# A new order of the same instructions on all five queues of a two-layer kernel

## The chip, the cores and the metric

The kernel runs on one core of one Trainium2 chip. The metric is the device time of one execution in microseconds (us). Before the change the median of three runs is 381.72 us (380.91 to 382.23).

## What is computed

Eight sequences of 256 tokens with 128 channels (2048 tokens) go through two layers. In short:

```python
xn = layernorm(x)                       # layer 0
q, k, v = xn@Wq+bq, xn@Wk+bk, xn@Wv+bv  # 16 query heads of 8, 4 key/value heads
x = x + (softmax(q k^T / sqrt(8)) v)@Wo + bo + (g1+g2) * (relu(xn@w1)@w2)   # top-2 gates, one shared expert
xn = layernorm(x)                       # layer 1: state-space block and ternary FFN
xs, z = split(xn@W_in);  xs = silu(causal_conv4(xs));  dt = softplus(xs@W_dt + b_dt);  Bs = xs@W_x
h_t = h_{t-1} * exp(-A dt_t) + Bs_t     # 256 channels x 16 states, scanned over the tokens
y = (sum_s h_t + D*xs) * silu(z)
f = silu(s1*xn@w1) * (s2*xn@w2);  f = gelu(h1s*f@h1);  f = gelu(h2s*f@h2)   # 128 -> 512 -> 512 -> 512
x = x + y@W_out + s3*f@w3
```

In the changed kernel nothing of this is computed in another way.

## The kernel before

Each engine runs one fixed list of *pieces*. A piece is a small function that waits for its semaphores and issues one to ten instructions. The lists stand in `ORDERS` (lines 72 to 126), one string per queue: `3*S` means three S pieces, and the n-th S in the string gets n as its argument. `run_order` (line 129) walks the string. An engine never leaves its list's order, so a piece that waits holds up everything behind it on its engine. A piece is named here with its number, from 0: second4, D39.

**Layer 0** works by batch b of 256 tokens (8 of them). TensorE (PE): `xn_transposes` (438), `project` (458), `v_gate` (429), `S` (317: scores for the row maxima, two 48-row matmuls of 256 columns, 16 a batch), `max_rows` (421), `A` (337: scores again, one 51-row matmul of 512 columns, on the other half of the array's rows), `pv` (349), `heads`, `back`, `proj_out` (the output projection), `ffn_in`, `ffn_out`. 44 `warm` pieces (450) are matmuls on a constant, whose results nobody uses. ScalarE (ACT): `E` (546), the Exp of an A bank; `qk_out`, `relu`, `xn_out`, `o_out`, `normalised`. VectorE (DVE): `M` (586), the maxima of an S bank. GpSimd (POOL): `G` (the gates), `qk_split`, `maxima_split`. SyncE: `put`, `fetch`, `stack` and `rows` move q, k and the maxima through HBM, `loads` brings in layer 1's weights; `decay_rates` on ACT (1085) needs the first two of these loads.

**Layer 1** works by group g of 512 tokens (4 of them). PE: `x_transposes`, `x_in` (917, four a group: xs and z), `ffn` (865, four), `wx` (930), `step_in` (939), `b` (855, 16 a group: one state's Bs spread over 128 partitions), `second` and `third` (882, 894, eight each: the two 512x512 products), `out` (950, six: y@W_out first, then the FFN's last product). ACT: `D` (1071, 32 a group: the decay exp(-A dt) of one state and one half of the channels), `dt`, `gelu`, `hid` (the two Gelus, four each a group), `sil`, `taps`, `gate_x`, `gate_z`, `x_out`, `normalise`, `deviation`. DVE: `scan` (1153, 16 a group, two scans each: one state), `conv` (1128, the other taps), `mul`, `zm`, `xm`, `residual1`. POOL: `add` (1201, 32 a group: sums the scanned states), `start` (1194, D*xs, two a group), `split` (1217), `y` (1209).

What ties the queues around the change, in lines of the kernel:

```python
reached(eng, g3_ok, g - 1, KC, 2 * c + 2 if g > 1 else KC)     # 873, ffn(g>0, c<2): ffn4 needs hid0 to hid3
reached(eng, scan, g, 2 * NS, 2 * s if g == 0 and s < NB1 else 2 * (s - 1))  # 862, b(s): scans up to s-2
reached(eng, add_ok, g, 2 * NS, 2 * (s + 1 - NPAIR))           # 1155, scan(s): adds of state s-4
reached(eng, conv, g, 6, 3 * c + 3)                            # 1021, gate_x(c) needs conv(c)
x_done(eng, g)                                                 # 1195, start: both gate_x of its group
z_done(eng, g + 2, 2)                                          # 953, first out of g: both z gates of g+2
reached(eng, y_ok, g, CI, CI)                                  # 957, first out of g: both y of g
```

Of the kernel before, what the change touches and what calls it, by code (L numbers as in the profile page):

```python
# [69 lines left out]


ORDERS = dict(
    sync="""x_in head constants0 2*x_in ffn_weights 3*put fetch stack 3*put fetch 2*put 3*rows loads put fetch stack
        2*put loads 3*rows put fetch stack loads put 3*rows 2*put stack fetch 3*rows stack 3*put fetch 3*rows
        loads 3*put stack fetch 3*rows stack 3*put fetch 3*rows stack 3*rows 8*out landed""",
    tensor="""9*warm xn_transposes warm project 2*warm v_gate 8*warm S ffn_in 2*warm xn_transposes S ffn_in 2*S project
        2*S warm 2*S 2*warm xn_transposes 2*S ffn_out 2*S warm project 2*warm 2*S ffn_in 2*S warm ffn_in
        xn_transposes max_rows 2*S 4*warm v_gate warm 2*S warm ffn_out A S A S 4*warm A S A S project A S A S
        4*warm S A S warm ffn_in S A S pv A S A S ffn_in A S A S max_rows ffn_out S A S pv A S v_gate A S A S pv
        A S A S pv 2*A 2*S heads A S A S pv xn_transposes back A S A S project S A S A proj_out ffn_in max_rows  # L80
        pv A S A S ffn_in A S A S pv A S A S ffn_out A S A S pv A S A S v_gate heads A S A pv A S A back
        xn_transposes A S A S pv A S A S proj_out project max_rows ffn_in A S A S pv A S A ffn_in A S A S pv A S
        v_gate ffn_out A S A S heads A S A pv 2*A S back xn_transposes A S pv A S A S ffn_in A S A S proj_out
        ffn_in max_rows A S project S A S 2*pv S A S A v_gate heads S A S A ffn_out A S A xn_transposes back A S
        A S pv A S A S project proj_out A S A S pv S A S A pv A S A S max_rows ffn_in pv 2*S ffn_in 2*S heads
        v_gate S 2*A S ffn_out S A S A back A S A S pv 2*A S proj_out A 2*S A pv A S A ffn_in max_rows 2*A 2*S
        v_gate ffn_in A S A S pv S A S A pv A S A S ffn_out heads A S A pv A S A S back x_transposes A S A pv A
        S A proj_out S A S A x_in A S A pv max_rows x_in ffn x_in pv A x_in A ffn A wx A ffn 2*step_in A heads b
        x_transposes ffn A pv A b x_in A x_in A second b second A x_in b A pv back A second b A second x_in b A
        wx A proj_out b pv A step_in 2*b pv step_in heads b second back b second b 2*second b proj_out third b  # L90
        2*third b third b third x_transposes third b third b third x_in b ffn b x_in ffn x_in b 2*ffn x_in wx
        2*second b out b step_in b out second b 4*out x_transposes b 2*second 2*b 2*second x_in second 2*b
        step_in 2*third b third b x_in b 2*third b 2*third b third x_in b ffn b ffn b x_in ffn 2*out ffn 2*b wx
        2*second b 3*out b second b 2*second b 2*second b out b second 2*step_in 2*b 2*third b third b 2*third
        2*b 3*third ffn b ffn b out ffn b ffn b 2*out b out 3*second b 2*second b 2*second b second b 2*out
        third b 2*third b third b 4*third 6*out""",
    scalar="""roots deviation0 normalised xn_out deviation0 wide_out own_keys qk_out own_keys normalised own_keys relu
        xn_out deviation0 gate_exp relu normalised own_keys qk_out xn_out qk_out relu normalised relu
        negated_maxima gate_exp xn_out 7*E qk_out E relu 2*E relu E negated_maxima E normalised 6*E o_out E
        gate_exp E decay_rates 2*E xn_out 2*E qk_out 2*E relu negated_maxima 2*E relu 2*E normalised 4*E o_out  # L100
        2*E gate_exp 5*E xn_out 3*E normalised negated_maxima relu 4*E relu E qk_out E o_out 4*E gate_exp 6*E
        relu 2*E xn_out negated_maxima relu 2*E qk_out o_out 4*E normalised gate_exp 3*E xn_out 9*E
        negated_maxima relu qk_out o_out relu deviation 2*E gate_exp 10*E negated_maxima relu 2*E relu 4*E o_out
        gate_exp 2*E normalise 6*E x_out 4*E taps E negated_maxima taps gate_x E sil gate_z gate_x 2*E gate_z
        sil E o_out E b_in normalise sil 2*dt D E D sil E x_out D E 2*D E D taps 3*D E D taps D E 2*D E 2*D
        gate_z E 2*gate_x E 2*D E gate_z 2*D E b_in D E 3*D gelu o_out gelu 2*dt 5*D 2*gelu 4*D deviation hid
        normalise hid D x_out 4*D 2*hid taps 2*D 2*sil taps normalise gate_z sil 2*gate_x sil D gate_z D b_in
        9*D dt 11*D x_out 2*D gelu taps 3*gelu D dt 8*D taps D hid D 3*hid gate_z gate_x 2*sil gate_x gate_z 4*D
        2*sil 6*D b_in 9*D 2*gelu 3*D 2*gelu 2*dt 12*D 2*hid D 2*hid 2*sil 4*D 2*sil 10*D 2*gelu 4*D 2*gelu
        2*hid D 2*hid""",  # L110
    vector="""ones moments inverse moments clear inverse moments first_split v_out 4*M gate_sum 6*M gate_norm 2*M gated
        2*M inverse 4*M v_out 4*M gate_sum 2*M gate_norm 2*M gated 15*M v_out 2*M heads gate_sum 2*M gate_norm
        2*M back_out gated M residual 10*M v_out M heads M gate_sum M back_out gate_norm 2*M gated M residual
        6*M v_out 3*M heads M gate_sum M gate_norm M gated 2*M back_out 2*M residual 5*M v_out 2*M heads M
        gate_sum back_out 2*M gate_norm 2*M gated 4*M residual 2*M statistics 5*M v_out heads 3*M gate_sum
        back_out M gate_norm 3*M gated 2*M residual 4*M inverse1 2*M v_out 2*M heads M gate_sum 3*M gate_norm
        back_out M residual 3*M gated 2*conv clear mul zm 2*xm zm 2*mul scan mul heads scan conv 2*scan conv
        scan zm back_out scan zm scan residual 2*scan heads clear 2*scan back_out scan residual scan statistics
        scan inverse1 4*scan conv scan 2*mul conv zm 2*mul scan zm 5*scan residual1 scan residual1 2*scan conv
        6*scan conv 2*scan zm 2*mul zm 2*scan 2*mul 6*scan 2*residual1 9*scan 2*mul 2*scan 2*mul 6*scan  # L120
        2*residual1 3*scan 2*residual1""",
    gpsimd="""ones biased 2*G biased 4*G qk_split 2*G qk_split maxima_split 8*G biased qk_split maxima_split 8*G
        maxima_split qk_split constants 8*G maxima_split G qk_split 7*G maxima_split qk_split 8*G maxima_split
        qk_split 8*G maxima_split 8*G maxima_split 2*start split 9*add start 3*add start 2*add split 18*add 2*y
        18*add start add split 2*add start 11*add 2*y 8*add 2*start 14*add split 11*add y 4*add y 26*add y add y""",
)


# [1213 lines left out]
```

## Time and profile before

| | |
|---|---|
| median of 3 runs | 381.72 us |
| the profiled execution | 380.91 us, of it 379.1 us span |
| busy share of the span | PE 97%, ACT 84%, DVE 80%, POOL 66% |
| granted TensorE clock, mean over the span | 1.000 |

Times are microseconds from the span's start. A row of a timeline gives start, duration from the first start to the last end, the line, the operation with its tiles, and how many instructions it merges; in square brackets stands the engine's idle time before it and who ended it. PE's ends are modelled and overlap, so its busy share does not show short waits; the starts do.

### The profile page before, as it was taken

The numbers are of one execution on the slowest core, as the hardware profiler recorded it, in microseconds if no ns is written. First come the engines' busy times: TensorE is split into PE (matmuls) and PEld (weight loads), VectorE is DVE, ScalarE is ACT, GpSimd is POOL, SyncE is SP. The second block draws the span as 40 slices with busy tenths as digits, with TensorE's granted clock in tenths as the row PEclk, the third lists the DMA queues.
The fourth block names the chain that finished last, engine by engine and source line by source line (L and its number), as shares of the span: only waits on it lengthen the run. The fifth ranks groups of instructions, "written<-read, shape, count | busy, mean of one in ns | idle before, by whom it ended". The sixth has DMA issues, their size and how long they took to land.

```text
span 379.1 us, 5770 instructions
## 1 busy us (share of the span) xinstructions
PE 367.3 (97%) x1762; PEld 184.9 (49%) x1762; DVE 303.6 (80%) x510; ACT 317.8 (84%) x541; POOL 251.5 (66%) x289
## 2 busy tenths in 40 slices
PE   7999999999999999999998999999999999899996
PEld 5667535455545453333344434754445544374445
DVE  4877888878788879469999889989999879786850
ACT  4924879787879797799999999999999999989440
POOL 2245814614515111637799993999999999998880
PEclk9999999999999999999999999999999999999999
DMA  5373975724555320000000000000000000000000
GB/s 212 91 146 116 176 179 159 129 56 103 155 118 108 69 41 3 0 2 1 0 0 3 1 0 0 2 28 1 1 2 0 0 29 3 0 0 1 29 0 28
DMA packets 27726, 18.84 MB, mean 50 GB/s; under 512 B 2832, under 2 KB 26672, under 8 KB 27440
## 3 DMA queue, kind: packets, MB, share of 16 engines
q1 hardware_dynamic: 27696, 18.48, 20.0%
q8 instruction: 14, 0.23, 0.3%
q14 instruction: 16, 0.13, 0.1%
HBM read 13.29 MB, written 4.98 MB: 48 GB/s over the span
## 4 chain that ended last, share of the span: by engine, by line
PE 38%; issue 32%; ACT 15%; POOL 12%; DVE 1%; DMA 1%; POOLq 1%; ACTq 0%; DVEq 0%
POOL acc L1207 8%; PE bank L360 7%; PE bank L345 5%; ACT da L1081 4%; PE bank L331 4%; PE bank L391 4%; PE bank L399 4%; ACT pt L551 3%; PE bank L454 2%; PE bank L320 2%; PE bank L460 1%; PE bank L927 1%; POOL y L1215 1%; PE bank L417 1%; PE bank L973 1%
## 5 line engine op out<-in xcount | busy, mean ns | idle before, releaser
L1207 POOL TENSOR_TENSOR acc<-acc,hb 128x512 f32<-128x512 f32 x128 | 158.3, 1275 | 20.5 <-DVE hb L1159 15.8
L1159 DVE TENSOR_TENSOR_SCAN hb<-da,bank 128x512 f32<-128x512 f32 x128 | 146.2, 1200 | 20.1 <-PE bank L863 15.7
L592 DVE TENSOR_REDUCE mx<-bank 128x2 f32<-128x512 f32 x128 | 83.6, 685 | 22.5 <-PE bank L331 18.5
L551 ACT ACTIVATE pt<-bank 128x512 f32<-128x512 f32 x128 | 71.4, 596 | 16.2 <-PE bank L345 13.8
L1081 ACT ACTIVATE da<-dt,nega 128x510 f32<-128x510 f32 x128 | 82.5, 714 | 0.2
L902 PE MATMUL bank<-gelu,ld 128*128 128x512 f32 x128 | 58.3, 593 | 1.1 <-ACT gelu L1062 1.1
L890 PE MATMUL bank<-sil,ld 128*128 128x512 f32 x128 | 58.7, 594 | 0.0
L345 PE MATMUL bank<-q_st,k_st 51*128 51x512 bf16 x128 | 42.5, 383 | 1.5 <-ACT pt L551 1.3
L331 PE MATMUL bank<-k_st,q_st 48*128 48x256 bf16 x240 | 39.3, 273 | 0.0
L902 PEld LDWEIGHTS bank<-gelu,ld 128*128 128x128 f32 x128 | 23.9, 190 | 27.9 <-issue 26.0
L890 PEld LDWEIGHTS bank<-sil,ld 128*128 128x128 f32 x128 | 23.9, 190 | 25.4 <-issue 24.0
L360 PE MATMUL bank<-pt,v_sb 128*32 128x512 f32 x256 | 33.9, 604 | 0.0
L345 PEld LDWEIGHTS bank<-q_st,k_st 51*128 51x128 bf16 x128 | 9.7, 93 | 38.2 <-ACT pt L551 30.5
L1081 ACT ACT_TABLE_LOAD x19 | 24.4, 1283 | 0.3
L863 PE MATMUL bank<-b_parts,sel 96*128 96x512 bf16 x64 | 23.4, 381 | 0.3 <-DVE hb L1159 0.3
L729 POOL TENSOR_TENSOR m_parts<-negm,m_parts 32x128 bf16<-32x128 f32 x8 | 3.3, 417 | 28.6 <-ACT negm L507 28.6
L331 PEld LDWEIGHTS bank<-k_st,q_st 48*128 48x128 bf16 x240 | 15.6, 94 | 9.6 <-DVE mx L592 4.7
L1135 DVE SCALAR_TENSOR_TENSOR xc<-bank,ld,xc 128x510 f32<-128x510 f32 (+2 forms) x24 | 17.8, 743 | 2.6 <-ACT xc L1008 2.0
L1069 ACT ACTIVATE gelu<-bank,ld 128x512 f32<-128x512 f32 x16 | 10.4, 684 | 9.5 <-PE bank L902 9.4
L706 POOL TENSOR_TENSOR gd<-srt 128x16 f32<-128x16 f32 x8 | 1.7, 215 | 24.4 <-issue 16.1
L879 PE MATMUL bank<-xnT,ld 128*128 128x512 f32 x32 | 16.8, 608 | 0.8 <-ACT gelu L1069 0.6
L391 PE MATMUL bank<-xnT,w 128*128 128x256 f32 x64 | 17.4, 394 | 0.1
(148 smaller groups left out, 580.1 us busy)
## 6 DMA issues: line engine op xcount, KB each, us to landing
q_st<-q_scr SPq DMA_DIRECT2D x8, 384.0 KB, 4.6
q_st<-q_scr SPq DMA_DIRECT2D x15, 192.0 KB, 4.0
ld<-in_pack SPq DMA_DIRECT2D x2, 1024.0 KB, 6.3
q_scr<-qk_parts SPq DMA_DIRECT2D x8, 192.0 KB, 2.4
k_st<-k_scr SPq DMA_DIRECT2D x15, 96.0 KB, 4.3
q_scr<-qk_parts SPq DMA_DIRECT2D x8, 128.0 KB, 1.8
out<-x SPq DMA_DIRECT2D x8, 128.0 KB, 1.9
ld<-in_pack SPq DMA_DIRECT2D x1, 968.0 KB, 5.7
```

What stands on the lines that cost most here:

```text
L331: last = mm(s_bank[n % 2][:, j * T:(j + 1) * T], q_st[b % 2][0:ROWS, 2 * pair + j, q * P:(q + 1) * P], k_st[b % 2][0:ROWS, 2 * pair // G, ...
L345: mm(st(b, n)[:, :], k_st[b % 2][HALF:, kv, kt * P:(kt + 1) * P], q_st[b % 2][HALF:, h0:h0 + 2, :].rearrange("r h n -> r (h n)"), start=Tr ...
L360: last = mm(pv_bank[kv * VW:(kv + 1) * VW, :], v_sb[b % 2][:, kt, kv, at:at + VW], pt[:, (4 * grp + kv) % 8, :], start=(grp == 0), stop=(g ...
L391: last = mm(bB[:, j * T:(j + 1) * T], w1[:, c * P:(c + 1) * P], xnT[b % 2][:, :], start=True, stop=True)
L551: act(pt[:, n % 8, :], st(b, n)[:, :], ACT.Exp, scale=HD ** -0.5).then_inc(p_ok, 1)
L592: eng.tensor_reduce(mx[:, 2 * pair:2 * pair + 2, q], s_bank[n % 2][:, :].rearrange("p (h k) -> p h k", h=2), AX.X, ALU.max).then_inc(mx_ok, 1)
L863: mm(b_bank(g, s)[:, :], sel[:, s, :], b_parts[:, g % 2, :], start=True, stop=True).then_inc(b_ps, 1)
L890: last = mm(f_bank(g, c)[:, :], h1[:, k, c * P:(c + 1) * P], sil[:, k, :], start=(k == 0), stop=(k == KC - 1))
L902: last = mm(f_bank(g, c)[:, :], h2[:, k, c * P:(c + 1) * P], g2[:, k, :], start=(k == 0), stop=(k == KC - 1))
L1081: act(da(n)[:, :, 1:T], dt[:, g % 2, c, :].rearrange("p (b n) -> p b n", b=GB)[:, :, 1:T], ACT.Exp, scale=nega[:, c, s:s + 1]).then_inc(da ...
L1159: eng.tensor_tensor_scan(hb[:, s % NPAIR, c, :], da(n).rearrange("p b n -> p (b n)"), b_bank(g, s)[:, :], 0.0, ALU.mult, ALU.add).then_inc ...
L1207: TT(acc[:, g % 2, c, :], acc[:, g % 2, c, :], hb[:, s % NPAIR, c, :], ALU.add).then_inc(add_ok, 1)
```

## The change

Only the strings of `ORDERS` differ. Every queue keeps exactly the same pieces in the same numbers (83, 612, 424, 305 and 232), and pieces of one name keep their order among themselves. No piece's code changes. Compared piece by piece, the stretches that the prediction speaks of, written out with their numbers (`-` before, `+` after; the lists themselves are too long to show whole):

```diff
 sync
- put8 fetch2 stack1 put9 put10 loads1 rows3 rows4 rows5 put11 fetch3 stack2 loads2
+ put8 stack1 fetch2 put9 put10 put11 rows3 rows4 rows5 loads1 stack2 fetch3 put12
 tensor (around 112 us)
- S99 ffn_in13 S100 S101 heads4 v_gate6 S102 A80 A81 S103 ffn_out6 S104 A82 S105 A83
+ ffn_in13 S99 S100 v_gate6 heads4 A80 S101 A81 S102 ffn_out6 S103 A82 S104 A83
 tensor (from 203 us)
- b12 proj_out7 third0 b13 third1 third2 b14 third3 b15 third4 x_transposes2 third5 b16 third6 b17 third7 x_in8 b18 ffn4 b19 x_in9 ffn5
+ proj_out7 third0 b12 third1 b13 third2 third3 b14 b15 third4 b16 third5 x_transposes2 b17 third6 third7 b18 x_in8 b19 x_in9 ffn4 b20 ffn5
- x_in11 wx2 second8 second9 b21 out0 b22 step_in4 b23 out1 second10 b24 out2 out3 out4 out5
+ x_in11 wx2 out0 out1 out2 b21 out3 out4 b22 out5 second8 b23 second9 second10 b24 step_in4
- third8 third9 b30 third10 b31 x_in13 b32 third11 third12 b33
+ b30 b31 third8 third9 b32 third10 third11 x_in13 b33 b34 third12
 scalar (before layer 1's first decays; then from 202 us)
- sil1 E114 o_out6 E115 b_in0 normalise1 sil2 dt0 dt1 D0
+ sil1 E113 b_in0 E114 E115 sil2 o_out6 dt0 dt1 D0
- D23 D24 D25 D26 D27 gelu2 gelu3 D28 D29 D30 D31 deviation1 hid0 normalise2 hid1 D32 x_out2 D33 D34 D35 D36 hid2 hid3
+ D23 D24 D25 D26 gelu2 gelu3 D27 D28 D29 D30 D31 D32 deviation1 hid0 hid1 D33 normalise2 D34 D35 D36 D37 D38 D39 x_out2 hid2 hid3
- taps4 D37 D38 sil4 sil5 taps5 normalise3 gate_z4 sil6 gate_x4 gate_x5 sil7 D39 gate_z5 D40 b_in2
+ taps4 taps5 sil4 sil5 normalise3 gate_x4 gate_z4 sil6 gate_x5 sil7 gate_z5 D40
 vector (around 112 us; then from 223 us)
- M96 M97 statistics0 M98 ... M102 v_out6 heads4 M103 ... M115 inverse10 M116
+ M96 statistics0 M97 ... M100 inverse10 v_out6 M101 heads4 M102
- scan17 conv4 scan18 mul4 mul5 conv5 zm4 mul6 mul7 scan19 zm5 scan20
+ scan17 scan18 conv4 mul4 mul5 conv5 zm4 mul6 mul7 zm5 scan19 scan20
 gpsimd (from 218 us)
- add31 y0 y1 add32 add33 add34 add35 add36 add37 add38 ... add49 start4 add50 split2 add51 add52 start5 add53
+ add31 add32 add33 add34 y0 add35 y1 start4 add36 ... add41 start5 add42 ... add49 split2 add50 add51 add52 add53
```

On PE everything from second23 on, to the last piece, stands as before. In front of out12 the same pieces stand in both lists.

## Rows read from the trace of the kernel before

**Rows 1.** The page's first part: busy us, share of the span, instructions of each engine.
```profile
PE 367.3 (97%) x1762; PEld 184.9 (49%) x1762; DVE 303.6 (80%) x510; ACT 317.8 (84%) x541; POOL 251.5 (66%) x289
```
**Rows 2.** Busy time by stretches: length, then each engine's busy us (instructions); clock, DMA.
```profile
160.00:180.00 20.00, 19.01 (x64) 6.66 (x63) 16.10 (x20) 19.94 (x33) 11.46 (x10) 1.00 0.00 1
220.00:240.00 20.00, 19.24 (x59) 9.11 (x58) 17.77 (x22) 19.90 (x32) 13.27 (x11) 1.00 0.00 0
260.00:280.00 20.00, 20.00 (x52) 8.75 (x51) 19.86 (x20) 19.82 (x26) 20.00 (x17) 1.00 0.00 0
```
**Rows 3.** Waits: engine, line and releaser: us in total, times, longest.
```profile
PEld bank L345 <- ACT pt L551: 30.5, 51, 1.2
POOL acc L1207 <- DVE hb L1159: 15.8, 11, 6.0
```
**Rows 4.** Timeline of PE: start, us, line, operation, count [idle before, releaser].
```profile
35.17 0.39 PE L345 MATMUL bank<-q_st,k_st 51*128 51x512 bf16 x1
35.17 0.39 PE L331 MATMUL bank<-k_st,q_st 48*128 48x256 bf16 x2
35.40 0.38 PE L345 MATMUL bank<-q_st,k_st 51*128 51x512 bf16 x1
35.71 1.05 PE L454 MATMUL bank<-warm_in 128*128 128x256 bf16 x8
...
204.73 1.98 PE L902 MATMUL bank<-gelu,ld 128*128 128x512 f32 x4 [1.09 <-ACT gelu L1062]
...
221.94 1.10 PE L879 MATMUL bank<-xnT,ld 128*128 128x512 f32 x2 [0.58 <-ACT gelu L1069]
...
227.94 1.13 PE L879 MATMUL bank<-xnT,ld 128*128 128x512 f32 x2 [0.18 <-DVE sil L1118]
...
265.21 0.38 PE L863 MATMUL bank<-b_parts,sel 96*128 96x512 bf16 x1
```
**Rows 5.** Timeline of PE, the end: the first out pieces of the last two groups.
```profile
329.57 0.38 PE L863 MATMUL bank<-b_parts,sel 96*128 96x512 bf16 x1
331.54 2.02 PE L963 MATMUL bank<-wout_half,y 128*128 128x128 f32 x16 [1.59 <-POOL y L1215]
...
370.65 2.02 PE L963 MATMUL bank<-wout_half,y 128*128 128x128 f32 x16 [0.41 <-POOL y L1215]
372.51 3.74 PE L973 MATMUL bank<-ld,gelu 128*128 128x128 f32 x32
```
**Rows 6.** Timeline of POOL.
```profile
234.54 2.65 POOL L1207 TENSOR_TENSOR acc<-acc,hb 128x512 f32<-128x512 f32 x2 [6.03 <-DVE hb L1159]
237.62 12.34 POOL L1207 TENSOR_TENSOR acc<-acc,hb 128x512 f32<-128x512 f32 x10 [0.44 <-DVE hb L1159]
249.95 1.55 POOL L1199 TENSOR_SCALAR acc<-xs,ld 128x512 f32<-128x512 f32 x1
...
330.01 1.28 POOL L1215 TENSOR_TENSOR y<-acc,zs 128x512 f32<-128x512 f32 x1
```
**Rows 7.** Timeline of ACT.
```profile
205.99 2.55 ACT L1081 ACTIVATE da<-dt,nega 128x510 f32<-128x510 f32 x4
...
220.53 1.26 ACT L1069 ACTIVATE gelu<-bank,ld 128x512 f32<-128x512 f32 x2
...
230.82 1.15 ACT L1026 ACTIVATE xs<-xc 128x512 f32<-128x512 f32 x2
231.86 0.69 ACT L1002 ACTIVATE sil<-bank,ld 128x512 f32<-128x512 f32 x1
232.57 1.28 ACT L1081 ACT_TABLE_LOAD   x1
233.86 0.72 ACT L1081 ACTIVATE da<-dt,nega 128x510 f32<-128x510 f32 x1
```
**Rows 8.** DMA issues near 44.9 us: size, us from issue to landing.
```profile
ld<-in_pack SPq DMA_DIRECT2D x1, 968.0 KB, 5.7
```
**Rows 9.** Timeline of ACT: the first reader of that load, in decay_rates0.
```profile
55.62 0.19 ACT L1092 ACTIVATE f_half<-ld 128x4 f32<-128x4 f32 x1
```

More of the change, by code:

```diff
@@ L72 @@
 ORDERS = dict(
[L73 to L125, printed above, removed]
+    sync="""x_in head constants0 2*x_in ffn_weights 3*put fetch stack 3*put fetch 2*put 3*rows loads put stack fetch
+        3*put 3*rows loads stack fetch put rows put 2*rows put stack fetch loads 3*rows put stack 2*put fetch
+        3*rows stack 3*put fetch loads 3*rows stack 3*put fetch 3*rows stack 3*rows 8*out landed""",
@@ new lines @@
+    scalar="""roots deviation0 normalised xn_out deviation0 wide_out 2*own_keys qk_out relu deviation0 normalised
+        2*own_keys xn_out gate_exp relu qk_out 2*normalised xn_out qk_out 2*relu negated_maxima gate_exp
+        normalised E xn_out 5*E qk_out 2*E relu 2*E relu E negated_maxima 7*E o_out E gate_exp E decay_rates 2*E
+        xn_out 2*E qk_out 2*E relu negated_maxima 2*E relu 3*E normalised 3*E o_out 2*E gate_exp 4*E xn_out 4*E
+        normalised negated_maxima 2*E relu 2*E relu E qk_out gate_exp E o_out 10*E normalised xn_out relu 2*E
+        negated_maxima 2*E relu qk_out gate_exp o_out 6*E xn_out 10*E relu negated_maxima qk_out o_out deviation
+        relu E gate_exp 9*E normalise 2*E negated_maxima relu 2*E relu 3*E normalise 2*E o_out gate_exp 7*E
+        x_out 2*E taps 3*E negated_maxima E taps gate_x sil gate_z E gate_x gate_z sil E b_in 2*E sil o_out 2*dt
+        D x_out E D sil E taps D E 2*D E 2*D taps 3*D E 3*D E 2*D E 2*D E gate_x gate_z gate_x E gate_z D E b_in
+        E 4*D E D 2*gelu dt o_out dt 4*D 2*gelu 6*D deviation 2*hid D normalise 6*D x_out 2*hid 2*taps 2*sil
+        normalise gate_x gate_z sil gate_x sil gate_z 15*D b_in 7*D dt D x_out 2*D 4*gelu dt 4*D taps 6*D 2*hid
+        taps 2*hid gate_x sil gate_z sil gate_x gate_z 3*D 2*sil 11*D b_in 4*D gelu 3*D 3*gelu 2*dt 12*D 2*hid D
+        2*hid 2*sil 4*D 2*sil 10*D 2*gelu 4*D 2*gelu 2*hid D 2*hid""",
@@ L126 @@
+    gpsimd="""ones biased G biased 4*G qk_split 3*G biased qk_split maxima_split 8*G qk_split maxima_split 8*G qk_split
+        maxima_split constants 8*G maxima_split 3*G qk_split 5*G maxima_split 3*G qk_split 5*G maxima_split
+        qk_split 8*G maxima_split 8*G maxima_split 2*start split 12*add start 2*add split 10*add start 11*add y
+        add y start 6*add start 8*add split 14*add y 4*add y 8*add start 3*add start 7*add split 11*add y 4*add
+        y 26*add y add y""",
 )
```

31 lines of the change are left out of this document (added).

## The prediction

> **What bounds the kernel now.** I read the page's busy times first, then the stretches, the waits, and the timelines of single queues. PE is busy for 97% of the span [rows 1], but ends are modelled, so I counted starts. Each instruction takes its columns at its own rate; what is left between two starts is a wait or a switch. From 206 to 366 us only three such waits are over 0.15 us: before 221.94, 227.94 and 331.54 [rows 4, 5]. At 260 to 280 us PE and POOL are both at 20.00 of 20 us and ACT at 19.82 [rows 2]: three queues are full at once, so nobody gains alone. Earlier, at 160 to 180 us, ACT is full (19.94) and PE is not; there A pieces wait for E pieces. Over the whole span A's weight loads wait 30.5 us for E, in 51 waits of at most 1.2 us, most of it while other matmuls still stream [rows 2, 3]. POOL has one large hole, 6.03 us before 234.54, and then adds almost without a stop [rows 3, 6]. The end tells the rest: out12 waits for POOL's y5 until 331.54, 1.75 us after b53 is over, and out18 waits for y7 until 370.65 [rows 5]. So PE and POOL arrive at the end nearly together, and from out12 on the two lists are the same on PE and have the same order on ACT, DVE and POOL.
>
> **What the new order can change.** The instructions are the same in number. PE's sum of work cannot move, only its waits and its switches; the same holds for POOL. I therefore follow four points: third0, ffn4, gate_x5 with start4, and out12.
>
> *PE's switches.* A on rows 64 up and S on the lower rows start together at 35.17, and the next A comes 0.23 us later; the warm matmul after them starts at 35.71, some 0.10 us after the second pair's 0.21 us are over [rows 4]. I take 0.1 us for each change between paired-row work and anything else. In front of out12 the old list has 177 such changes (pv's included), the new one 174: -0.3 us. A's and S's that stand in a row without a partner are one fewer: -0.2 us. Together -0.5 us, of which -0.4 lies before step_in0.
>
> *0 to 157 us.* first_split0 comes behind M0 and qk_out0 behind own_keys1, so batch 0's q and k reach HBM some 1.2 us later; S8 stood 2 us behind their landing, so this is covered. inverse2 comes earlier and xn_out2 waits for it (about 0.6 us at project2), but M14 and M15 lose the 0.9 us that inverse2 took from them, so max_rows0 comes out even within 0.2 us. loads1 moves behind rows3 to rows5, from 44.9 to about 49.2 us. It needs 5.7 us [rows 8], lands near 54.9, and its first reader stood at 55.62 [rows 9]: covered by 0.7 us. If the cover is gone, ACT waits, and behind it E20 and so A22. Bounds 0 to 1.5 us (the 960 KB of stack2 and fetch3 now follow it closely); I take 0, since it is first in the queue. inverse10 moves ahead of v_out6, behind deviation0 with its table load, and holds M101, heads4 and M102; S104 waits for M102. By the starts that is 0.8 us, but the old order had 0.9 us of waits at A82 to A85: 0, bounds -0.5 to +1. Sum to step_in0: -0.4, bounds -1.5 to +2.
>
> *D0 to third0.* normalise1 (1.6 us) is gone from in front of sil2, and o_out6 (0.6 us) comes in; with PE 0.4 us earlier, D0 comes 0.7 us earlier. Before gelu2 stand four decays of group 0 since dt3 instead of five. A decay costs 0.61 us: four take 2.55 us and the last of them 0.72 [rows 7]. So gelu3 ends 1.3 us earlier. third0 waited 1.09 us for it [rows 4] and will wait less; it comes 1.3 us earlier, near 203.4.
>
> *third0 to ffn4.* This goes the other way. Between gelu3 and hid3 ACT had nine decays (D28 to D36) and gets thirteen (D27 to D39): 4 x 0.61 = +2.45 us. hid3 ended at 221.79 [rows 7] and will end at 221.79 - 1.3 + 2.45 = 222.9. ffn4 waited 0.58 us for it already [rows 4] and moves from 221.94 to 223.05: +1.1. Everything on PE is queued behind it. Part is used: b19 and x_in9 now stand ahead of ffn4 and fill 1.1 us, so PE's later work is no later than before.
>
> *ffn4 to start4.* From hid3 to gate_x5's end ACT sheds a table load and two decays. A load stands in the trace for 1.28 us, and from sil7's start to D39's it is 2.00 us where 0.55 is usual, so 1.45 us in all [rows 7]. 1.45 + 2 x 0.61 = 2.7 us less; sil5 waits 0.4 us for the later ffn5. gate_x5 ended at 231.97 [rows 7] and will end at 231.97 + 1.15 - 2.7 + 0.4 = 230.8 by ACT, 231.2 with conv5's chain, which is near it on DVE. I take 231.2.
>
> *POOL.* start4 is put before add36 and waits for gate_x5; behind it are queued all adds. The hole stays, and moves to before start4. From 231.2: start4 1.55, two adds 2.45 (an add is 1.23 us: ten take 12.34 [rows 6]), then add38 at 235.3 instead of 234.54. But start4 is now done, 1.55 us that stood at 249.95, and the pauses of 0.44 and 0.11 us behind add38 don't come back, as the scans are ahead. 235.3 - 234.54 - 1.55 - 0.55 = -1.35 us. y5 ends at 331.29 [rows 6] and will end at 329.9.
>
> *Does PE arrive too?* It was ready for out12 at 329.8 [rows 5]. +1.1 at ffn4, -1.1 for the two pieces ahead, -0.35 for the old wait before 227.94 (0.18 us of it shown as idle [rows 4]), +0.25 at x_transposes3, which now meets a later dt4: 329.7. One more wait is added: b30 and b31 stand before third8, b31 5.6 us of PE work earlier than in the old list, where it started at 265.21 [rows 4]. It needs scan29, which needs add51. By POOL's count add51 ends at 257.7 and scan29 at 260.0, just when PE comes there. Cost 0; bounds 0 to 1.5. So out12 starts 0.25 us after y5, at 330.2 instead of 331.54.
>
> **Sum.** -1.35 us; after out12 all four queues repeat the old order. The profiled execution would take 380.91 - 1.3 = 379.6. The median shown is 0.8 us above that execution, so against the median I predict 381.72 - 1.3 = 380.4 us.
>
> The whole new ACT list has 46 table loads instead of 50, 4 x 1.45 = 5.8 us less. I give nothing for the other three: they lie after 243 us, where ACT is ahead of POOL's adds and PE shows no wait for it.
>
> The Trainium skill (ScalarE: Activation LUTs, What ACT_TABLE_LOAD costs) puts a switch of sets at about 2.66 us, 1283 ns of load and 1380 ns of drain. The trace has the load but not such a drain. By the page gate_x5 would come 1.2 us earlier still and the sum would be near -2.5; by the row it stays at -1.35, and the row decides.
>
> **Rivals.**
> *More is gained: the waits of the merged stage shrink.* Between 157 and 206 us PE loses about 5.5 us in waits for E, gate_z, gelu. The new list spreads A120 to A127 wider among second, x_in and step_in. If half of these waits go and ACT follows, then D0, gelu3 and with them hid3 and gate_x5 come 2 us earlier again; y5 would end at 328, PE would be the later one at out12 (1.75 + 0.5 us to win), and the 0.58 us before out18 would go as well. -3.5 us: 378.2. Against it: ACT is full there [rows 2], so E pieces can't come sooner than the decays beside them allow.
> *No change.* POOL's hole ends by DVE: conv5, then zm and mul, and scan19 behind zm5 in both lists. If conv5 ends no sooner than before, start4 gives back what the hole took, and out12 stays near 331.5: 0 to -0.5 us, 381.5.
> *Slower: start4 holds POOL.* Place: start4 before add36. In the old order add36 and add37 ran before the hole without waiting for any gate. Now they and all later adds stand behind gate_x5, which stands behind hid3, thirteen decays, ffn4, sil, conv5. The point of decision: y5 comes as before when gate_x5 ends at 231.2 + 1.35 = 232.5; each microsecond more is one at the end. If D0's 0.7 us and the 0.6 us before gelu2 don't come and loads1 or inverse10 costs its bound, gate_x5 ends near 234.2, and b31 waits for scan29 by as much: +1.7 us, 383.4. For it: three links of this chain are added waits. Against it: ACT's shed work of 2.7 us is counted from rows.
>
> **How the numbers follow.** Forecast 0.43, its own range 379.4 to 381.4; more gained 0.18; no change 0.16; slower 0.23. For 8 in 10 I reach to the middle of the first rival and to the price of the last: 377.8 to 383.4. No change within 0.3% (1.15 us) is what a measurement here can't tell. Faster by more is all of the first rival and six tenths of the forecast: 0.44. Slower by more is most of the last: 0.21. The rest is 0.35.
>
> **What would show it.** Right: third0 near 203.4 with a wait under 1 us; ffn4 later than 222.5, waiting for hid3; POOL's hole before a TENSOR_SCALAR (start4), ended near 231.3 by ACT; add38 near 235.3; out12 near 330.2, released by y5; out18 still released by y7, the last matmuls unchanged behind it; 46 table loads. Wrong: ffn4 without a wait or before 221.5 (first rival); b31 with a wait over 1 us, ffn_out or A22 late by over 1 us near 56 us, or start4 after 232.5 (last rival). The step that I trust least is the count of ACT's work between third0 and gate_x5, since it leans on ACT never waiting there.

## The result, and the profile after

The changed kernel takes 384.41 us (median of 8 runs, 382.89 to 384.49), the kernel before took 381.98 us in the same series (8 runs). The ratio is 1.0054 with a 95% interval of 1.0031 to 1.0077: about 2.1 us slower. I had forecast 1.3 us faster and a range that ended at 383.4. The profiled execution took 384.20 us, 3.3 more than that of before. Why the two profiles stand further apart than the ratio is told in the last section: the profile of before was a fortunate execution.

The page's busy times [rows 1], of the changed kernel. Its line numbers are one lower than those of before.

```profile
PE 370.4 (97%) x1762; PEld 186.2 (49%) x1762; DVE 305.4 (80%) x510; ACT 312.6 (82%) x537; POOL 251.8 (66%) x289
```
ACT issues 537 instructions instead of 541 and is busy 5.2 us less: the four table loads are gone as counted. POOL does the same work.

The stretch of [rows 2] in which three queues had been full, after the change:

```profile
260.00:280.00 20.00, 19.38 (x49) 8.41 (x48) 16.57 (x16) 16.54 (x24) 19.95 (x17) 1.00 0.00 0
```
ACT fell from 19.82 to 16.54 us and DVE from 19.86 to 16.57; POOL is still full. ACT and DVE have room there now, POOL has none.

Waits, the lines that answer to [rows 3], and one more of each kernel: weight loads of S pieces that wait for DVE's maxima (the first two and the last line are of the changed kernel, the third is of before, 35 to 158 us; the changed kernel has 6.4 us in that stretch too).

```profile
PEld bank L344 <- ACT pt L550: 27.7, 46, 1.1
PEld bank L330 <- DVE mx L591: 6.4, 15, 0.8
...
PEld bank L331 <- DVE mx L592: 4.7, 10, 0.8
...
POOL acc L1206 <- DVE hb L1158: 11.0, 11, 1.9
```
Waits for the Exp became fewer and waits for the maxima more. Many of these lie beside matmuls that still stream, so they don't say what PE loses; the table at mhalf_old, which goes by starts, does.

PE's timeline at the points of [rows 4, 5]:

```profile
206.37 1.99 PE L901 MATMUL bank<-gelu,ld 128*128 128x512 f32 x4 [0.34 <-ACT gelu L1061]
...
215.17 1.96 PE L901 MATMUL bank<-gelu,ld 128*128 128x512 f32 x4 [0.78 <-ACT gelu L1068]
...
220.71 0.66 PE L913 MATMUL bank<-head,xn 128*128 128x128 f32 x4 [1.65 <-ACT xn L1034]
...
227.53 1.10 PE L878 MATMUL bank<-xnT,ld 128*128 128x512 f32 x2 [0.33 <-ACT gelu L1068]
...
265.02 0.39 PE L862 MATMUL bank<-b_parts,sel 96*128 96x512 bf16 x1 [0.62 <-DVE hb L1158]
...
334.65 0.38 PE L862 MATMUL bank<-b_parts,sel 96*128 96x512 bf16 x1
334.87 1.97 PE L962 MATMUL bank<-wout_half,y 128*128 128x128 f32 x16
...
373.92 2.02 PE L962 MATMUL bank<-wout_half,y 128*128 128x128 f32 x16 [0.41 <-POOL y L1214]
```
These are third0, third4, x_transposes2, ffn4, b31, the last b before out12 (b53), out12 and out18. Three waits are new: 0.78 us before third4, for ACT's hid0, 1.65 before x_transposes2, for ACT's normalise2, and 0.62 before b31. The wait of 1.59 us before out12 is gone, and yet out12 starts 3.3 us later: it follows b53 by 0.22 us, the usual distance behind a b, so PE itself arrives last.

POOL [rows 6], ACT [rows 7] and DVE around it:

```profile
235.91 1.57 POOL L1198 TENSOR_SCALAR acc<-xs,ld 128x512 f32<-128x512 f32 x1 [5.91 <-ACT xs L1025]
```
```profile
219.01 1.65 ACT L1034 ACTIVATE xn<-x,nmean,rstd 128x128 f32<-128x128 f32 x4 [1.38 <-DVE nmean L1149]
220.56 3.76 ACT L1080 ACTIVATE da<-dt,nega 128x510 f32<-128x510 f32 x6
...
226.12 1.27 ACT L1068 ACTIVATE gelu<-bank,ld 128x512 f32<-128x512 f32 x2
...
235.18 0.63 ACT L1025 ACTIVATE xs<-xc 128x512 f32<-128x512 f32 x1
```
```profile
214.21 2.33 DVE L1158 TENSOR_TENSOR_SCAN hb<-da,bank 128x512 f32<-128x512 f32 x2 [0.75 <-PE bank L862]
216.45 0.18 DVE L1147 RECIPROCAL rstd<-std 128x8 f32<-128x8 f32 x1
216.66 2.25 DVE L1149 SCALAR_TENSOR_TENSOR nmean<-mv,rstd 128x8 f32<-128x8 f32 x1
```
POOL's hole is where I had put it, before start4. ACT waits 1.38 us in front of normalise2, which I had not in the sum.

### The profile page after: what moved, and what is told of

The parts are those of the page before. It is cut to its first block and busy times, and to the rows that moved or that the text cites. A ratio compares the mean times of both kernels' runs of the same rounds, so it can differ in the third digit from the quotient of the medians.

```text
span 382.4 us, 5766 instructions
## 1 busy us (share of the span) xinstructions
PE 370.4 (97%) x1762; PEld 186.2 (49%) x1762; DVE 305.4 (80%) x510; ACT 312.6 (82%) x537; POOL 251.8 (66%) x289
## 5 line engine op out<-in xcount | busy, mean ns | idle before, releaser
L1068 ACT ACTIVATE gelu<-bank,ld 128x512 f32<-128x512 f32 x16 | 10.5, 685 | 13.8 <-PE bank L901 13.7
L972 PEld LDWEIGHTS bank<-ld,gelu 128*128 128x128 f32 x128 | 15.9, 192 | 2.7 <-issue 2.5
```

What stands on the lines that cost most here:

```text
L972: last = mm(out_bank(g, q)[:, r], g3[:, k, r], w3[:, k, :], start=False, stop=(k == KC - 1 and q == out_last(g, q)))
```

## The experiments

In all tables step_in0 (PE, the end of layer 0's own stretch) and out12 are starts in the profiled execution. "Before" is the kernel before in the same series. The medians are over all executions of a kernel, of which the profile shows one.

A single step_in0 can mislead by 2 us: with the head of before it stands between 158.0 and 160.0 in seven profiles, by the start of the kernel and by the fetches of q and k (last section). So I also give a *clean distance*: from the start of A0 to that of step_in0, less the waits of PE's weight loads for the fetch (`PEld ... <- DMA q_st`). It is 122.5 to 122.7 us in these seven, 124.6 to 124.7 in the three profiles with the new head (changed, new_head, inv_early): the new head is 2.1 us longer.

| lists | this | before | ratio (95%) | step_in0 | out12 |
|---|---|---|---|---|---|
| before, first profile | | 381.72 | | 158.0 | 331.5 |
| changed | 384.41 | 381.98 | 1.0054 (1.0031 to 1.0077) | 160.3 | 334.9 |
| new_head | 384.40 | 382.33 | 1.0045 (1.0024 to 1.0066) | 159.9 | 333.4 |
| new_tail | 382.84 | 382.33 | 1.0006 (0.9988 to 1.0025) | 158.9 | 333.6 |
| inv_early | 383.47 | 382.33 | 1.0034 (1.0013 to 1.0055) | 160.1 | 334.1 |
| to86 | 382.66 | 382.33 | 1.0011 (0.9990 to 1.0032) | 158.9 | 332.4 |
| old_inv10 | 381.38 | 381.49 | 1.0004 (0.9986 to 1.0023) | 158.1 | 331.7 |
| to116 | 384.71 | 381.49 | 1.0083 (1.0060 to 1.0107) | 161.0 | 334.6 |
| tail_heads7 | 383.94 | 381.49 | 1.0062 (1.0039 to 1.0084) | 158.2 | 333.6 |
| tail_b31 | 387.28 | 381.49 | 1.0144 (1.0117 to 1.0171) | 158.8 | 338.7 |
| start4_hole | 379.61 | 382.31 | 0.9957 (0.9933 to 0.9980) | 159.6 | 331.7 |
| mid_old | 383.31 | 382.31 | 1.0025 (0.9998 to 1.0052) | 160.3 | 333.7 |
| pe_mid_new | 387.25 | 382.31 | 1.0112 (1.0067 to 1.0157) | 163.4 | 338.7 |
| mid_new | 388.42 | 382.31 | 1.0146 (1.0093 to 1.0198) | 167.8 | 341.3 |
| dve_old | 391.68 | 382.50 | 1.0228 (1.0191 to 1.0264) | 167.5 | 341.0 |
| best2 | 380.51 | 382.50 | 0.9956 (0.9929 to 0.9982) | 160.0 | 332.2 |
| mhalf_old | 381.20 | 381.87 | 0.9967 (0.9935 to 1.0000) | 156.5 | 330.1 |
| mhalf_new | 382.85 | 381.87 | 1.0022 (0.9993 to 1.0051) | 161.3 | 334.8 |
| tail_inv | 381.69 | 381.87 | 0.9988 (0.9962 to 1.0014) | 158.1 | 332.1 |

**new_head and new_tail: which half.** The lists are cut where both have done the same pieces, at step_in0.

```diff
 every queue
- old pieces up to step_in0, old behind it
+ new_head: new up to step_in0, old behind it; new_tail: the reverse
```


> New lists up to step_in0 (PE 399, ACT 203, DVE 198, POOL 85, SyncE 59 pieces), the lists of before behind it. Theory H (the loss is made in layer 0): the changed kernel has step_in0 2.3 us later than before, and out12 only 3.3 later, so this kernel should have step_in0 near 160.3 us (before 158.0) and carry it through to the end, +2.0 to +2.4 us on the kernel before. Rival T (the loss is made in the merged stage at 200 to 230 us, and the wait of 1.75 us at out12 would absorb a late layer 0): step_in0 late, but the end within +0.7 us.

> The lists of before up to step_in0, the new lists behind it. Theory H: the rest costs what is left of +2.4 us, about +0.2 to +0.6 us. Rival T: ffn4 is as late against D0 as in the changed kernel (61.5 us behind D0 instead of 58.1), and the end comes +1.5 to +2.5 us. My forecast on record had -1.0 us for this part (its -1.35 less the 0.4 us of layer 0).

Theory H holds for the larger part. The new head alone costs +0.45%, 1.7 us (0.9 to 2.5), and carries its lateness to the end; the medians show no cost of the new tail (+0.2 us, -0.5 to +1.0). In the profiles step_in0 to out12 takes 173.5 us before, 174.6 with the new tail, 174.6 in the changed kernel, so there the tail costs 1.1 us, just outside that interval, and ffn4 comes 61.5 us behind D0 in new_tail, as rival T said. The tail's share of the loss is thus 0.2 to 1.1 us; in no reading does it bring the -1.0 us that I had forecast for it.

**inv_early and tail_inv: inverse11.**

```diff
 vector (inv_early on the changed lists, tail_inv on old head and new tail)
- scan13 scan14 inverse11 scan15
+ scan13 inverse11 scan14 scan15
```


> The new lists with one exchange on DVE: inverse11 ahead of scan14, as before the change. Theory T1: normalise2 was late (219.0 instead of 212.05) because inverse11 stood behind scan14, and scan14 waited for b14, which now stands behind third3; then normalise2 comes about 2.2 us earlier, x_transposes2 loses its wait of 1.8 us, ffn4 comes 0 to 1 us earlier, and the end is 0 to 1 us earlier than in the changed kernel. Rival A1: ffn4 waits for hid3, and ACT's thirteen decays set hid3 whatever DVE does; then x_transposes2 moves and ffn4 and the end don't (within 0.3 us of the changed kernel, +2 on the kernel before).

> The lists of before up to step_in0, the new ones behind it, with inverse11 ahead of scan14. From the pieces of the earlier runs: step_in0 to out12 took 173.5 us before the change, 174.6 with the new tail, 174.0 with the new lists and early inverse11. Theory (each part of the tail is independent of the head): 173.9 to 174.1 here, the end +0.4 us on before. Rival: the head's lateness had covered a wait of the tail, and the distance is 174.4 or more.

inv_early has normalise2 at 217.38 instead of 219.01, with no idle time before it (the first row below follows D33 at once), hid3 ends at 225.73 instead of 227.38 (second row: hid2 and hid3). Step_in0 to out12 falls from 174.6 to 174.0 us, and ffn4 comes 0.5 us earlier against D0; the ratios, 1.0054 and 1.0034, can't be told apart. In tail_inv the same distance is 174.05, as expected: in the profiles the parts add up. Its end did not come 0.4 us late as expected; the ratio 0.9988 is no difference from before. My detail on x_transposes2 was wrong: it came only 0.1 us earlier. PE's wait did not go, it moved ahead: b16 waits 1.69 us for scan14, which now stands behind inverse11 and its long nmean (third row, PE).

```profile
217.38 1.63 ACT L1037 ACTIVATE xn<-x,nmean,rstd 128x128 f32<-128x128 f32 x4
...
224.47 1.26 ACT L1071 ACTIVATE gelu<-bank,ld 128x512 f32<-128x512 f32 x2
```
```profile
218.65 0.38 PE L865 MATMUL bank<-b_parts,sel 96*128 96x512 bf16 x1 [1.69 <-DVE hb L1161]
```

**to86, old_inv10, to116, mid_old: where in layer 0.** to86 has the new lists up to A51 (86 us), to116 up to S99; mid_old is new_head with the stretch from A51 to pv19 (86 to 112 us) as before.

```diff
 vector (old_inv10, on the lists of before)
- M102 v_out6 heads4 M103 ... M115 inverse10 M116
+ M102 inverse10 v_out6 heads4 M103 ... M115 M116
```


> New lists only up to A51 (PE's first 202 pieces, about 86 us), the lists of before behind it. In the changed kernel A48 is 1.3 us late and A112 2.4 us. Theory H1 (the loss builds up piece by piece): about half of layer 0's loss, step_in0 +1.2 to +1.4, the end about +1.2 us. Rival H2 (the old list behind 86 us takes it back, since E and A have slack there): step_in0 within 0.4 us of before and the end within 0.4 us.

> The lists of before with one piece moved: DVE's inverse10 stands ahead of v_out6 (112 us) instead of behind M115. Theory I (this move makes part of layer 0's loss): inverse10 waits for ACT's deviation0 and its table load and holds M103 and heads4, so S104 waits and step_in0 comes 0.5 to 1.0 us later, with it the end. Rival N (my step on record, cost 0): step_in0 at 158.0 to 158.9 as in other runs of this head, the end within 0.3 us of before.

> New lists up to PE's piece 301 (S99, about 114 us), the old lists behind it; inverse10 stands late, as before the change. Step_in0 was at 158.0 (before), 158.9 (new up to 86 us), 159.9 (new up to 158 us). Theory B (the A pieces in runs of four without filler, A51 to A55 at 88 us and A65 to A70 at 104 us, run into the Exp rate of ACT): step_in0 at 159.4 to 159.8, with waits at A67, A68 and S88 of 0.2 to 0.5 us each. Theory I: the loss lies behind 116 us, step_in0 at 158.8 to 159.0 and the end about +0.4 us.

> New lists up to step_in0, but the stretch from 86 to 112 us (A51 to pv19, on all four engines) as before the change; the old lists behind step_in0. The new lists for all of layer 0 had step_in0 at 159.9 and the end +1.7 us. Theory B (in this stretch the new list takes v_gate5 and ffn_out5 ahead of A64, so A64 to A70 stand in a row and run into ACT's rate of one Exp in 0.49 us, with S88 behind them): step_in0 0.8 to 1.1 us earlier, 158.8 to 159.1, and the end +0.6 to +0.9 us. Rival D (the loss is spread evenly): 0.2 to 0.4 us earlier.

The clean distances are 122.9 us in old_inv10, 123.6 in to86, 125.0 in to116 and 124.3 in mid_old. So moving inverse10 costs 0.2 to 0.4 us at most, and nothing at the end, within what my prediction had for it (0, bounds -0.5 to +1). to86 has 1.0 of the new head's 2.1 us: about half of the loss is made before 86 us, as theory H1 said, though of its end the measurement sees only 0.4 us (-0.4 to +1.2). to116 has the waits that theory B named (A68 0.43, S88 0.47 us), but a seam of its own too, 0.73 us before S99. mid_old does not bear out theory B: it takes back 0.3 to 0.4 us, not 0.8 to 1.1, which is rival D's size. (Its step_in0 of 160.25 says less, as 0.6 us of it are a wait for the fetch.) The waits of A pieces in that stretch did fall, from 2.4 to 1.5 us, but S waits behind it and the list's own length took most of the gain back; the ratios 1.0045 and 1.0025 can't be told apart.

**pe_mid_new, mid_new, dve_old: one queue's list at a time.** pe_mid_new changes only PE's order from 86 to 112 us on the old lists, mid_new that stretch on all queues, dve_old gives new_head DVE's old order from M18 to M98.

> The lists of before, PE alone with the new order from 86 to 112 us. Theory B: waits at A67, A68 and S88 of 0.2 to 0.5 us as in the changed kernel, step_in0 at 158.8 to 159.8 and the end +0.8 to +1.0 us. Rival E (it is the place of the other engines' pieces, v_out5, heads3 and qk_out6, that makes the waits): step_in0 within 0.3 us of 158.0 or 158.9.

> The lists of before with the new order from 86 to 112 us on all engines. Theory B: step_in0 0.9 to 1.1 us later, the end +0.9 to +1.1 us. Rival D: +0.2 to +0.4 us.

> New lists up to step_in0 and old lists behind it, as in the run of the new head (step_in0 at 159.9, end +1.7 us), but DVE's pieces from M18 to M98 (30 to 116 us) in the order of before. In the new head PE loses 3.8 us in front of S pieces that wait for M (before the change 2.0), in front of A pieces 6.4 (before 5.5 to 6.1). Theory M (DVE's new order, with heads, gate_norm and gated ahead of M pieces, makes the waits of S): S's waits fall to 2.2 to 3.0 us, step_in0 0.8 to 1.6 us earlier, the end +0.2 to +0.9 us. Rival P (PE's own order makes them: S stands nearer to the M that frees its bank): S's waits stay at 3.5 us or grow, step_in0 at 159.5 or later, the end +1.4 us or more.

All three are far slower than any theory said and tell nothing of the question. The mixed lists open one or two long waits: PE is idle for 1.61 us before back3 in pe_mid_new, for 1.89 before S76 in mid_new, for 2.66 before heads3 and 1.61 before back3 in dve_old. In the ten microseconds around and behind them the granted clock is below 1: 0.80 and 0.86 in pe_mid_new, 0.60 and 0.72 in mid_new. (2 us of mid_new's late step_in0 are its slow start, see the last section.) In dve_old heads3, and window rows as in [rows 2]:

```profile
106.69 0.63 PE L379 MATMUL bank<-head,o_sb 128*128 128x128 f32 x4 [2.66 <-ACT o_sb L496]
```
```profile
105.00:110.00 5.00, 1.88 (x11) 0.75 (x11) 2.12 (x8) 3.36 (x7) 3.86 (x6) 0.84 0.21 55
110.00:115.00 5.00, 4.47 (x23) 1.77 (x24) 2.15 (x6) 1.36 (x3) 0.67 (x4) 0.50 0.41 106
```
The granted clock of 0.50 is the lower of the two levels, 1.2 GHz.

**mhalf_old and mhalf_new: are the waits for maxima the cause?**

```diff
-            eng.tensor_reduce(mx[...], s_bank[n % 2][:, :].rearrange("p (h k) -> p h k", h=2),
+            eng.tensor_reduce(mx[...], s_bank[n % 2][:, :].rearrange("p (h k) -> p h k", h=2)[:, :, 0:P],
```


> The lists of before; each M piece on DVE takes the maxima over the first 128 of 256 keys only (the rest is left out), so an M should take about 0.42 us instead of 0.69. Before step_in0 PE loses 2.0 us in front of S pieces, 5.5 to 6.1 in front of A pieces. Theory M (S waits are DVE's M two pieces back; DVE's share sets them): S's waits fall under 1 us, step_in0 comes 0.5 to 1.5 us earlier than in the same list with whole M pieces. Rival E (ACT's Exp sets the pace, S's waits only stand in for A's): A's waits grow by what S's lose, step_in0 within 0.4 us.

> The new lists up to step_in0 and the old behind it, with the same halved M pieces. PE lost 3.8 us in front of S, 6.4 in front of A there, and step_in0 stood 1.9 us later than before (fetch waits left out of both). Theory M: both heads now wait little for M, so the distance between the two heads falls from 1.9 us to 0 to 0.8 us. Rival E: the distance stays at 1.5 to 2.0 us, as the A waits take over.

An M piece falls from 684 to 419 ns. To compare heads I counted PE's loss: each piece at the rate of its columns, what is left between two starts is lost, and goes to the piece behind it (us up to step_in0; "first S": the first of a batch, which waits for the fetch of q and k; start: all up to 35 us):

| lists | list itself | A | S | first S | start | step_in0 less first S and start |
|---|---|---|---|---|---|---|
| before | 141.5 | 5.9 | 2.0 | 0.2 | 4.0 | 153.8 |
| new_head | 141.1 | 6.4 | 3.8 | 0.4 | 4.1 | 155.5 |
| mhalf_old | 141.5 | 6.3 | 1.2 | 0.2 | 3.8 | 152.6 |
| mhalf_new | 141.1 | 7.2 | 1.8 | 0.9 | 6.4 | 154.1 |

Both heads gain 1.2 to 1.4 us by this count, but their distance stays: 1.7 us with whole, 1.5 us with halved maxima. The profile of new_head shows no wait for the fetch, so its 0.4 in "first S" is rather PE's own; by the clean distance the heads are 2.1 us apart with whole and 1.5 with halved maxima (121.3 and 122.8 us). Theory M had 0 to 0.8, rival E 1.5 to 2.0. The medians differ by 1.65 us, as those of new_head and before by the ratio. So most of the distance does not hang on the length of M, as rival E said. Its reason holds only in part: the A pieces take over 0.4 of the 0.8 us that S loses in mhalf_old and 0.8 of 2.0 in mhalf_new, and step_in0 came 1.2 us earlier in mhalf_old, as theory M had it and not rival E. That the new order of PE's pieces waits more for whichever of M and E is late fits all this, but no run shows it alone.

**start4_hole: POOL's part alone.**

```diff
 gpsimd (on the lists of before)
- add36 add37 add38 ... add49 start4 add50
+ add36 add37 start4 add38 ... add49 add50
```


> The lists of before with one piece moved: POOL's start4 stands between add37 and add38, in POOL's hole of 228.5 to 234.5 us, instead of behind add49. It needs gate_x5 (ended 231.97) and takes 1.55 us, so it is over at 233.6, before add38 at 234.54. Theory S (y5 sets out12; this was the gain my forecast counted for POOL): y5 ends 1.5 to 2.1 us earlier, out12 loses its wait of 1.75 us, PE is then last: the end -1.5 to -2.3 us. Rival: what POOL gains is given back in scans and adds further on, as PE and DVE are the limit at 260 to 320 us: y5 -0.3 or less, the end within 0.5 us.

This kernel is faster than both: ratio 0.9957. POOL and PE in it:

```profile
227.62 2.50 POOL L1209 TENSOR_TENSOR acc<-acc,hb 128x512 f32<-128x512 f32 x2
233.69 1.57 POOL L1201 TENSOR_SCALAR acc<-xs,ld 128x512 f32<-128x512 f32 x1 [3.56 <-ACT xs L1028]
236.16 2.65 POOL L1209 TENSOR_TENSOR acc<-acc,hb 128x512 f32<-128x512 f32 x2 [0.91 <-DVE hb L1161]
```
```profile
331.20 0.38 PE L865 MATMUL bank<-b_parts,sel 96*128 96x512 bf16 x1
331.72 2.02 PE L965 MATMUL bank<-wout_half,y 128*128 128x128 f32 x16
```
start4 lies wholly in the hole, and add38 still waits 0.91 us behind it for its scan. out12 starts 0.52 us behind b53, where 0.22 is usual, so 0.3 of its wait of 1.75 us is left. From D0 (165.41 here, 163.84 before) out12 comes 166.31 us later instead of 167.70, 1.39 less. Theory S holds in kind; its size for y5 (1.5 to 2.1 us) was a little too large, and the end is 1.65 us earlier by the ratio (0.8 to 2.6).

**best2: the two decays.**

```diff
 scalar (on start4_hole)
- D26 D27 gelu2 gelu3 D28 ... D35 D36 hid2 hid3 taps4 D37
+ D26 gelu2 gelu3 D27 D28 ... D35 hid2 hid3 taps4 D36 D37
```


> The lists of before with start4 in POOL's hole (which took 379.6 us, -1.65 us and more), and on ACT D27 behind gelu3 instead of ahead of gelu2, D36 behind taps4 instead of ahead of hid2. Theory G (PE's waits of 1.26 us before third0 and 0.75 us before ffn4 are ACT's gelu3 and hid3, a decay of 0.61 us less ahead of each): third0 and ffn4 0.6 us earlier against D0, and the end up to 0.6 us earlier if POOL's adds come too. Rival Y (POOL's y5 and DVE's scans now set out12 together with PE): third0 and ffn4 0.6 us earlier, out12 and the end within 0.2 us of the kernel with start4 alone.

From D0, third0 comes 40.30 us later instead of 40.91 in start4_hole, ffn4 57.52 instead of 58.13: 0.61 us each, one decay, as counted. out12 comes 166.28 later instead of 166.31: rival Y. POOL got nothing from it, as D36 only moved from in front of hid2 to in front of gate_x5: gate_x5 ends 68.27 us behind D0 instead of 68.18, y5 166.02 instead of 166.05, and out12 again starts 0.26 us behind y5. So here a wait removed on PE alone bought nothing, as y5 still arrived last.

**tail_heads7 and tail_b31.**

```diff
 tensor (tail_heads7, on new_tail; DVE's heads7, back_out7, inverse11 as before too)
- A127 b7 step_in3 pv31 b8 second4 b9 second5 b10 second6 b11 heads7 second7 back7 proj_out7
+ A127 b7 b8 pv31 step_in3 heads7 b9 second4 back7 b10 second5 b11 second6 second7 proj_out7
 tensor (tail_b31, besides)
- b28 second14 b29 second15 step_in5 x_in12 b30 b31 third8 third9 b32 third10 third11 x_in13
+ second14 x_in12 second15 b28 b29 step_in5 third8 third9 b30 third10 b31 x_in13 b32 third11
```


> The lists of before up to step_in0, the new ones behind it, but with heads7 and back7 on PE and heads7, back_out7 and inverse11 on DVE where they stood before. In the run of the new tail normalise2 came at 217.7 (before 212.05) and the distance from step_in0 to out12 was 174.6 instead of 173.5 us. Theory T2: late heads7 delays back_out7, residual7 and scan11, and with them scan14, inverse11 and normalise2; then normalise2 comes at 214 to 215, x_transposes2 waits under 0.5 us, and step_in0 to out12 is 173.0 to 173.6 (the end -0.5 to +0.3 us of before). Rival A1: hid3 and ffn4 are set by ACT's thirteen decays alone: ffn4 stays within 0.4 us of the new tail with early inverse11 (66.7 us behind step_in0), and the end likewise.

> As the kernel with heads7 in its old place, and besides b30 and b31 behind third8 and third10 as before the change. In the new tail b31 waits 0.8 us for scan29. Theory P (PE arrives last at out12 in the new tail, so each wait on it counts): the end 0.5 to 0.8 us earlier than with heads7 alone. Rival Q (POOL's adds set y5 and out12, b31's wait lies beside it): the end within 0.2 us of it.

Both experiments failed on the same ground: a piece set back to its old place on PE meets partners that the new lists have later. Early heads7 waits for ACT's o_out7, 2.46 us of idle PE. The last Exp has long ended (191.7), but the new ACT list has o_out7 behind gelu1 and dt2, where it stood between the two Gelus before:

```profile
196.77 0.59 ACT L496 ACTIVATE o_sb<-bank 128x512 f32<-128x512 f32 x1
```
tail_b31 moved more than its expectation says: b28 and b29 too stand later on PE, as before the change. b29 comes at 262.94 instead of 258.31 in tail_heads7, the scans behind it are as late, and b34, which in the new lists stands right behind b33, waits for scan32 (ended at 275.50). So neither P nor Q was tested:

```profile
273.33 0.39 PE L865 MATMUL bank<-b_parts,sel 96*128 96x512 bf16 x1
275.56 0.39 PE L865 MATMUL bank<-b_parts,sel 96*128 96x512 bf16 x1 [1.83 <-DVE hb L1161]
275.78 5.29 PE L904 MATMUL bank<-gelu,ld 128*128 128x512 f32 x8
```
```profile
275.00:280.00 5.00, 4.45 (x7) 1.94 (x8) 5.00 (x6) 2.19 (x4) 5.00 (x5) 0.66 0.00 0
```
After 1.83 us of idle PE the granted clock is 0.66 over five microseconds, and eight matmuls take 5.29 us; the same eight (same line of code) take 3.60 us in the changed kernel:

```profile
221.44 3.60 PE L901 MATMUL bank<-gelu,ld 128*128 128x512 f32 x8
```

## Why the prediction was wrong

The chain of my sum, link by link, from the two profiles (us):

| link | before | after | change | forecast |
|---|---|---|---|---|
| start to D0 | 163.84 | 166.02 | +2.2 | -0.7 |
| D0 to gelu3's end | 40.84 | 40.30 | -0.5 | -0.6 |
| gelu3 to hid3's end | 17.11 | 21.06 | +4.0 | +2.45 |
| hid3 to gate_x5's end | 10.18 | 8.43 | -1.75 | -1.9 |
| gate_x5's end to add38 | 2.57 | 4.10 | +1.5 | +1.5 |
| add38 to y5's end | 96.75 | 94.63 | -2.1 | -2.15 |

The last column's sum is -1.4, the measured one +3.3. Two links failed, and they are 4.4 of the 4.7 us between the two. By the medians the loss is +2.1 us, of it 1.7 in the head.

*0 to 157 us, "Sum to step_in0: -0.4, bounds -1.5 to +2".* This is the step that failed most. PE's list became shorter by 0.4 us as I counted, inverse10 cost next to nothing (old_inv10), the first batch cost nothing (A0 in new_head at 35.19 against 35.17), and loads1 neither (its reader in decay_rates0 starts at 56.26 with no wait before it). But I had argued each moved piece by itself and never walked PE's new list against the Exp and the maxima that each A and S needs two pieces back. A pieces waited 0.5 us more and S pieces 1.8 us more by the count of the table at mhalf_old. Measured alone, this is +1.7 us by the ratio and +2.1 by the clean distance. The causes that I had offered for a late head (loads1, inverse10) were not it. What exactly in the order makes the waits is open: about half of them come before 86 us (to86), the stretch from 86 to 112 us carries a fifth at most (mid_old), and most does not hang on the length of the maxima (mhalf_old, mhalf_new).

*third0 to ffn4, "Between gelu3 and hid3 ACT had nine decays and gets thirteen: +2.45".* The count was right: with inverse11 early the link takes 19.57 us (206.16 to 225.73) instead of 17.11, which is +2.46. What I missed is that ACT would wait: normalise2 stood behind inverse11, inverse11 was put behind scan14, scan14 behind b14, which went behind third3. I had written that I trusted this count least "since it leans on ACT never waiting there"; it waited 1.38 us. And inverse11 was not only late but long, its nmean 2.25 instead of 0.72 us (last section).

*D0 to third0; ffn4 to start4; POOL.* Right, each within 0.2 us. The hole ended by start4, two adds and add38 as counted. That start4 in the hole is worth 1.4 us is shown alone by start4_hole; the change gave it together with add36 and add37, which had not waited before and now did. From gate_x5's end to y5's it is 99.3 us before, 97.9 in start4_hole and 98.8 in the changed kernel: 0.9 of the 1.4 us went back so, and the rest and more by gate_x5, which ends 1.7 us later against D0. No run parts start4 from the two adds.

*"Does PE arrive too?"* This failed as well, hidden by the chain above. I had PE ready for out12 at 329.7, which is 166.6 us behind D0, 0.6 more than before. It was ready 168.9 us behind D0, 2.9 more. Two of the waits that it met I had not looked at: before third4 (0.78 us, for hid0, with six decays between gelu3 and it instead of four) and before x_transposes2 (1.65). And b31, at cost 0, waited 0.62, within its bounds. out12 starts when PE is there, 0.31 us behind y5, where it starts 0.26 behind y5 when y5 is last (before, start4_hole). So PE and POOL are late by the same amount, within 0.05 us.

*The table loads.* The rule of the Trainium skill (ScalarE: Activation LUTs, What ACT_TABLE_LOAD costs), which would have had gate_x5 another 1.2 us earlier, is not borne out. In both profiles the activation behind a load starts 12 ns after the load's end and the load 17 to 18 ns after the activation ahead of it, with no drain on either side; hid3 to gate_x5 gave 1.75 us where the row's price gave 1.9. (That link alone would not decide it, as gate_x5 stands close behind conv5 on DVE, which ends at 235.14.)

*The end.* gate_x5 ended at 235.81, beyond the point of 232.5 from which my slower rival decides. By that rival's rule the end would be 235.81 - 232.5 = +3.3 us, which is what the profiles show. Its mechanism (start4 and all adds behind a late gate_x5) was there; I had given it 0.23. Its conditions came only in part: D0 did come late, but the 0.6 us before gelu2 did come and neither loads1 nor inverse10 cost its bound. That its rule gives the measured number is partly luck, since PE's own waits would have given the same end.

## What to carry to other kernels

Where engines run fixed lists in lock step, price a new list by walking it whole, each piece against the two or three that it waits for; counts on one engine are exact only if that engine never waits, so ask of every step in the chain what it waits for in the new list. A block moved into an existing hole pays (start4, -0.43%), the same block placed ahead of work that did not wait before gave most of it back. A list taken from one schedule does not go with lists from another: the hybrids here cost up to 2.3%, with waits of 1.6 to 2.7 us and a lower granted clock around and behind them. And before two single profiles are compared, take out what differs between executions of the same list: here the start and the fetches, up to 2 us each, as large as the effect.
